# A gated cross-attention and mixture-of-experts layer on one core: the calls of four engines are put in another order

## What is computed

```python
A   = sigmoid(sim) * (sim >= k_th_largest_of_row(sim, 153))      # sim from ctx, Wq, Wk: 512 x 512
adj = (1 - g) * layernorm(x) + g * 0.5 * (A + A.T)
x1  = x + tanh(gx) * adj
xn  = layernorm(x1)
probs = softmax(xn @ gate_w); take the best two of 8 experts per row, weigh them
h   = gelu(xn @ fc1[e] + b1[e]);  y = h @ fc2[e] + b2[e]          # per expert
out = x1 + tanh(gf) * sum over the two experts of weight * alpha[e] * y
```

## Time and profile before

| What | Value |
|---|---|
| Median of 3 runs | 364.33 us (362.4 to 364.58) |
| Profiled execution, its own time | 362.98 us |
| Span of that execution | 361.2 us |
| Mean granted TensorE clock | 0.956 |
| Busy share PE, PEld, DVE, ACT, POOL | 90%, 65%, 55%, 46%, 28% |

### The profile page before, as it was taken

The page is one execution under the profiler, slowest core; times in us unless marked ns, Lnnn a source line. Parts: engine busy times, 40 slices in busy tenths (PEclk is TensorE's granted clock), DMA queues, the critical chain, the costliest instruction groups (busy, mean ns, idle before and its releaser), DMA issues.

```text
span 361.2 us, 6213 instructions
## 1 busy us (share of the span) xinstructions
PE 324.1 (90%) x1969; PEld 234.2 (65%) x1969; DVE 200.2 (55%) x697; ACT 165.2 (46%) x384; POOL 100.0 (28%) x141
## 2 busy tenths in 40 slices
PE   7626998969999998999999989999999999999970
PEld 6303774867765865668868576777785867587720
DVE  0788798887878787698885372636206112311010
ACT  2776336489987656057786222232222212231320
POOL 5001011450111266214307413222733111312131
PEclk9956898989999999999999999999999999999995
DMA  3999999958965686866527766854688955544243
GB/s 91 381 392 362 363 360 382 367 185 189 301 121 154 133 243 210 154 133 197 103 54 188 193 144 139 205 117 91 197 169 153 172 125 105 107 69 86 31 69 54
DMA packets 53637, 65.81 MB, mean 182 GB/s; under 512 B 9792, under 2 KB 28512, under 8 KB 53600
## 3 DMA queue, kind: packets, MB, share of 16 engines
q1 hardware_dynamic: 46144, 47.99, 43.8%
q0 software_dynamic: 7456, 17.37, 24.9%
HBM read 39.56 MB, written 25.78 MB: 181 GB/s over the span
## 4 chain that ended last, share of the span: by engine, by line
PE 44%; issue 19%; DMA 10%; DVE 9%; POOL 5%; ACT 4%; DVEq 3%; POOLq 2%; SPq 1%; ACTq 0%
PE ps L1711 18%; PE ps L1684 14%; PE ps L1694 10%; POOL xs_rows L566 4%; DMA out_rows<-ab,dst 3%; DMA xs_rows<-ab,pos 2%; DMA xg_r<-xs_rows 2%; DMA meta<-xs_rows 2%; ACT ab L692 2%; DMA out_rows<-ys,dst 1%; ACT xb L722 1%; SPq L397 1%; PE ps L1721 1%; PE ps L1647 1%; POOLq L530 1%
## 5 line engine op out<-in xcount | busy, mean ns | idle before, releaser
L1684 PE MATMUL ps<-xgT_r,weights 128*128 128x128 f32 x768 | 91.6, 279 | 6.0 <-ACT xgT_r L743 3.5
L1684 PEld LDWEIGHTS ps<-xgT_r,weights 128*128 128x128 f32 x768 | 89.6, 195 | 11.0 <-issue 8.3
L1711 PE MATMUL ps<-weights,act_r 128*128 128x512 f32 x192 | 86.1, 595 | 1.2 <-ACT act_r L766 1.2
L580 POOL DMA_INDIRECT out_rows<-ys,dst x24 | 37.6, 1568 | 119.1 <-ACT ys L773 64.9
L1711 PEld LDWEIGHTS ps<-weights,act_r 128*128 128x128 f32 x192 | 34.9, 190 | 38.0 <-issue 36.5
L766 ACT ACTIVATE act_r<-ps,b1T 128x128 f32<-128x128 f32 x96 | 27.3, 366 | 37.8 <-PE ps L1684 37.7
L1694 PEld LDWEIGHTS ps<-sim,weights 128*128 128x128 f32 x256 | 35.2, 190 | 1.9 <-issue 1.9
L566 POOL DMA_INDIRECT xs_rows<-ab,pos x32 | 32.0, 1001 | 14.5 <-issue 9.1
L1694 PE MATMUL ps<-sim,weights 128*128 128x160 f32 x256 | 35.6, 299 | 0.0
L773 ACT ACTIVATE ys<-ys,meta 128x512 f32<-128x512 f32 x24 | 17.3, 719 | 34.7 <-DVE ys L1322 34.7
L1711 PE MATMUL ps<-weights,xb 128*128 128x512 f32 x64 | 28.1, 592 | 0.0
(11 more groups left out here) (206 smaller groups left out, 417.8 us busy)
## 6 DMA issues: line engine op xcount, KB each, us to landing
weights<-in_L_ffn_fc_w SPq DMA_DIRECT2D x16, 1024.0 KB, 8.7
b_r<-in_L_ffn_fc_b SPq DMA_DIRECT2D x32, 256.0 KB, 4.0
xg_r<-xs_rows SPq DMA_DIRECT2D x88, 64.0 KB
xb<-in_x SPq DMA_DIRECT2D x4, 1024.0 KB, 7.2
out_rows<-xb SPq DMA_DIRECT2D x4, 1024.0 KB, 5.9
sim<-xs_rows SPq DMA_DIRECT2D x32, 80.0 KB
xs_rows<-weights SPq DMA_DIRECT2D x1, 2064.0 KB, 13.1
xs_rows<-weights SPq DMA_DIRECT2D x2, 516.0 KB, 5.8
```

The lines of the kernel that those rows point to most:

```text
L580: pool.indirect_dma_start(out=out_rows, out_offset=bass.IndirectOffsetOnAxis(ap=dst[:, k % 2, e:e + 1], axis=0), in_=result_rows(m), in_of ...
L1684: mm = pe.matmul(ps[:, n % 2, i * P:(i + 1) * P], weights[:, e, 0, h, i * P:(i + 1) * P], rows[:, h * P:(h + 1) * P], start=(h == 0), stop ...
L1711: mm = pe.matmul(ps[:, 2 + m % 2, :], rows, weights[:, e, 1, i, :], start=(i == 0), stop=(i == IB - 1))
```

## The change

The lists of DVE, ACT, POOL and SP are replaced by others with the same calls; on PE nothing moves. Loops over the four tiles are written out so that calls can stand between them. Parts of the heads of the four lists (SP, POOL, ACT, DVE):

```diff
             load_b2(0, 0)
+            store_x1(0)
+            load_weights(6)
+            load_weights(7)
+            load_x(2)
+            load_meta(0)
             load_b2(0, 1)
-            store_x1(0)
-            fill_pads()
-            load_weights(6)
-            load_x(2)
-            load_weights(7)
-            load_meta(0)
             load_rows(0, 2)
             load_rows(0, 3)
+            fill_pads()
             fill_ends()
             load_rows(0, 4)
+            load_rows(0, 5)
+            load_rows(0, 6)
             load_b2(0, 2)
-            load_rows(0, 5)
             load_b2(0, 3)
-            load_rows(0, 6)
+            load_rows(0, 7)
             load_b2(0, 4)
             store_x1(1)
+            load_x(3)
             load_b2(0, 5)
-            load_rows(0, 7)
-            load_x(3)
             load_b2(0, 6)
+            load_rows(1, 0)
+            load_rows(1, 1)
+            load_rows(1, 2)
+            load_meta(1)
             load_b2(0, 7)
             load_b2(1, 0)
-            load_meta(1)
-            for t in range(3):
-                load_rows(1, t)
...
             rstd_of_x(0)
             rstd_of_x1(0)
+            scatter_rows(0, 0)
+            scatter_rows(0, 1)
+            scatter_rows(0, 2)
+            scatter_rows(0, 3)
             rstd_of_x(1)
-            for t in range(BT):
-                scatter_rows(0, t)
-            rstd_of_x(2)
-            for t in range(3):
-                add_result(0, t)
+            add_result(0, 0)
+            add_result(0, 1)
+            add_result(0, 2)
             rstd_of_x1(1)
             add_result(0, 3)
+            rstd_of_x(2)
+            scatter_rows(1, 0)
+            scatter_rows(1, 1)
+            scatter_rows(1, 2)
+            scatter_rows(1, 3)
             add_result(0, 4)
-            for t in range(BT):
-                scatter_rows(1, t)
             add_result(0, 5)
             add_result(0, 6)
             add_result(0, 7)
+            rstd_of_x1(2)
             add_result(1, 0)
+            add_result(1, 1)
             rstd_of_x(3)
-            rstd_of_x1(2)
...
             act.wait_ge(m_ps, 1)
             act.copy(m_qk[:], ps[:, 0, 0:C]).then_inc(m_sb, 1)
             context(0)
+            query(0)
+            scores(0, 0)
+            scores(0, 1)
+            scores(0, 2)
+            scores(0, 3)
+            squash(0, 0)
+            context(1)
             tanh_coefs()
-            query(0)
-            for t in range(BT):
-                scores(0, t)
-            for t in range(BT):
-                squash(0, t)
-            keep_b1()
             signs(0, 0)
+            signs(0, 1)
+            signs(0, 2)
+            squash(0, 1)
+            squash(0, 2)
+            query(1)
+            squash(0, 3)
             halve(0, 0)
...
-                turned(0, t)
+            turned(0, 0)
+            turned(0, 1)
+            turned(0, 2)
+            turned(0, 3)
             norm_plain(0)
+            signs(1, 0)
             norm_plain(1)
+            scores(2, 0)
+            keep_b1()
+            leaning(0)
+            scores(2, 1)
+            scores(2, 2)
             norm_plain(2)
             norm_plain(3)
-            scores(2, 0)
-            scores(2, 1)
-            leaning(0)
-            scores(2, 2)
             scores(2, 3)
             context(3)
-            for t in range(BT):
-                affine_x(1, t)
-            query(3)
-            signs(1, 0)
+            signs(1, 1)
             picked(0)
             picked(1)
-            signs(1, 1)
+            signs(1, 2)
             gelu(0, 0)
-            signs(1, 2)
+            candidates(1, 0)
+            candidates(1, 1)
+            query(3)
             gelu(0, 1)
+            candidates(1, 2)
+            candidates(1, 3)
+            squash(1, 0)
             signs(2, 0)
...
+            sim_stats(0, 0)
+            sim_stats(0, 1)
+            x_stats(0, 0)
+            sim_stats(0, 2)
+            sim_stats(0, 3)
+            first_guess(0)
+            count(0, 0)
+            narrow(0, 0)
             coefficients()
-            x_stats(0, 0)
-            for t in range(BT):
-                sim_stats(0, t)
-            first_guess(0)
-            keep_gate_sum()
-            count(0, 0)
-            x_stats(0, 1)
-            narrow(0, 0)
             count(0, 1)
-            x_stats(0, 2)
             narrow(0, 1)
             count(0, 2)
+            x_stats(0, 1)
+            x_stats(0, 2)
             x_stats(0, 3)
+            narrow(0, 2)
             x_var(0)
-            narrow(0, 2)
+            keep_gate_sum()
+            largest(0, 0)
+            largest(0, 1)
+            largest(0, 2)
+            largest(0, 3)
...
+            add(0, 2)
+            add(0, 3)
+            x1_stats(0, 0)
+            x1_stats(0, 1)
+            sim_stats(1, 2)
+            x1_stats(0, 2)
+            x1_stats(0, 3)
+            sim_stats(1, 3)
             x1_var_of(0)
-            x_stats(1, 2)
-            x_stats(1, 3)
+            first_guess(1)
             norm_bias(0)
+            best_two(0)
             norm(0, 0)
             norm(0, 1)
-            best_two(0)
             norm(0, 2)
             norm(0, 3)
-            x_var(1)
-            sim_stats(1, 0)
+            one_hot(0)
             gaps(0)
-            sim_stats(1, 1)
-            one_hot(0)
+            sim_stats(2, 0)
+            one_hot(1)
             shares(0)
-            one_hot(1)
             places(0)
-            next_places(0)
-            x_scales(1)
-            sim_stats(1, 2)
-            sim_stats(1, 3)
-            first_guess(1)
-            for t in range(BT):
-                sim_stats(2, t)
+            sim_stats(2, 1)
+            sim_stats(2, 2)
+            sim_stats(2, 3)
             first_guess(2)
             narrow(1, 0)
-            for t in range(BT):
-                x_stats(2, t)
-            x_var(2)
+            x_stats(1, 0)
...
```

462 lines of the change are left out of this document (257 added, 205 removed).

## The result

The changed kernel takes 374.45 us (median of 4 runs, 373.6 to 376.31), the kernel before 363.67 (362.4 to 364.58). The ratio is 1.0299 with an interval of 1.0257 to 1.0340: 3% slower, where 365 was forecast and 369.5 was the end of the range. The profiled execution took 373.6; its span is 371.8, 10.6 longer than before. In the experiments, times are medians of all runs, while ratios leave out the profiled execution and runs more than 1.5% above the fastest of the rest.

What follows compares the result with a forecast made beforehand. PE, busy for 90% of the span, was taken as the bound. Terms -2.3 - 1.6 + 6.1 - 1.6 + 0.9 = +1.5 gave 364.5 from the profiled 362.98, 365.8 from the median; predicted 365 us, range 360 to 369.5.

Steps and rivals of the forecast that it cites:

- part 2: From the first expert product to batch 1's first product: late POOL adds and scatter turn PE's -3.9 us into +2.2.
- part 1: Up to the first expert product at 75.21: start 2.3 us earlier, full clock saves 1.6, PE 3.9 ahead.
- part 3: From 149.57 to 212.12: windows turned before PE asks, so the 1.64 us gap goes, leaving PE at +0.6.
- part 4: From 212.12 to the end: layer2(2, 7) waits 0.9 us because add_bias(21) stands behind turn_rows(3, 0); +0.9.
- the sign: At batch 1's first product: PE 5 us or more behind would show that the landings failed.
- The price of the drain: On POOL ahead of batch 1's scatter: rstd_of_x(2)'s drain waits 5.9 us for the add's landing; bounds 0 and 7.87.
- The start of the adds: On POOL before batch 1's scatter: third add at 114.4 instead of 113.72, fourth at about 126.8.
- lead of 2.7 us: PE's 3.9 us lead from the head, about 1.2 of it lost by the transposed tile after layer2(0, 4).
- B: Adds between 113 and 150 land in 7.87 us, batch 1's product 4 to 6 later: 369 to 371; chance 0.17.
- C: Clock falls again behind the new 3.3 us gap at batch 1's products: 1.6 us, giving 366.6; chance 0.15.
- D: Lists don't do what the title says: copies precede affine passes but stay behind two counts; no separate chance.
- Catch up by the sixth add: Near the end: POOL's adds are one later and catch up by the sixth add of batch 3.

Runs made afterwards that it cites:

- e1: Changed kernel with rstd_of_x(2) moved back behind rstd_of_x(1) on POOL, ahead of the fourth add; 373.49 us, ratio 1.0236.
- e8: e1 with load_meta(3) ahead of store_x1(3) on SP and targets(3) ahead of add_bias(24) on DVE; 369.1 us, ratio 1.0155.
- e11: Changed kernel with only load_meta(3) ahead of store_x1(3) on SP and targets(3) ahead of add_bias(24) on DVE; 374.24 us, ratio 1.0297.
- e14: Changed kernel with narrow(2, 1) ahead of turn_rows(0, 4) on DVE; 376.3 us, ratio 1.0330.
- e3: Changed kernel with 20 matmuls on constants between the second and third transposed tile of adjacency(1, t) on PE; 377.04 us, ratio 1.0343.
- e4: Changed kernel with add_bias(21) moved back ahead of turn_rows(3, 0) on DVE; 377.37 us, ratio 1.0372.
- e10: Changed kernel with ACT's head reordered: norm_plain and two scores calls ahead of signs(1, 0), two picked calls ahead of signs(1, 1); 374.34 us, one run.
- e7: Kernel before with a bare POOL drain added between add_result(0, 4) and the scatter of batch 1; 368.56 us, ratio 1.0164.
- e13: Changed kernel with the first four weigh calls, weigh(0, 0) to weigh(0, 3), moved earlier on ACT; 371.24 us, ratio 1.0146.
- e15: Changed kernel with the moves of both e13 and e14; 368.84 us, ratio 1.0111.

## Why the prediction was wrong

The step that failed is the walk of POOL's adds in part 2 ("I walk to 114.4", "`add_result(0, 3)` starts at about 126.8", "the scatter starts at **132.7**"). Its mechanism was right and shown: the drain of `rstd_of_x(2)` waits for the fourth add, the scatter is late, PE idles. Its sizes were not. The scatter started at 138.01, 5.3 us later than forecast; from there to the product it took the 19.06 us of the forecast. So part 2's term, +6.1 in the sum, came out at +9.4 (from -1.95 at `layer2(0, 0)` to +7.5 at `layer1(1, 0)`). The sum also lacked a lower clock behind that (+1.7), and the other parts missed by less: part 1 gave -1.95 instead of -3.9, part 3 -0.6 instead of -1.6, part 4 +1.9 instead of +0.9. The prediction had named the sign: PE 5 us or more behind at that point means that the landings failed.

- **The price of the drain, 3.7 of the 5.3 us.** I took 5.9 after an add's start. The bare drain took 5.98, but in the changed kernel it was 9.59, since the add landed in 8.6 us; the slowest of the 34 adds before the change took 7.1 (the one at 202.44). Why this one took 8.6 stays open. The load of x beside it isn't enough: in the kernel before, the same load went out 1.48 us behind the same add (121.54), and that add landed in 4.9. The transfers there from 121 to 126:

```profile
xb<-in_x SPq DMA_DIRECT2D x1, 1024.0 KB, 6.8
out_rows<-ys,dst POOLq DMA_INDIRECT x1, 4.9
```

  In the new order the load goes out 1.09 us behind the add, with two bias loads behind it, and in e1, e8, e11 and e14, where that is the same, the add took 7.2 to 7.5. What of this makes it slow was not tried apart.
- **The start of the adds, 1.6 of the 5.3 us.** The third came at 117.06 instead of 114.4, the fourth at 128.42 instead of 126.8. Both rows name ACT, and no landing, as what ended POOL's wait, so that the first add came 8.7 us later than before held up neither. `weigh(0, 2)` waited behind the copy (L743) of a transposed tile, and that for PE, on whose lead of 2.7 us (3.9 less 1.2) the walk counted there. PE came to the tile at 114.94 and before the change at 115.01: 2.0 us of the lead had not been won in part 1, and the way to the tile had cost 1.9 instead of 1.2, the gap above all. From the third add the delay passed on to `leaning(1)`, which ran at 127.32 instead of 125.6, and with it to the fourth. PE before and after, and ACT after:

```profile
115.01 1.04 PE L1639 MATMUL ps<-ident,xb 128*128 128x128 f32 x8
```

```profile
114.94 1.06 PE L1717 MATMUL ps<-ident,xb 128*128 128x128 f32 x8
```

```profile
115.57 0.58 ACT L743 COPY x1T<-ps 128x512 f32<-128x512 f32 x1 [5.30 <-PE ps L1717]
116.06 0.72 ACT L786 ACTIVATE ys<-ys,meta 128x512 f32<-128x512 f32 x1
...
127.32 0.21 ACT L760 ACTIVATE lean<-gap 128x4 f32<-128x4 f32 x1 [5.13 <-DVEq L1238]
```

- **Rivals B and C came together with the forecast's mechanism.** I gave each a chance as if only one could come. B (a landing over 6.8 us) took place at the one landing that mattered; three adds of the kernel before had already been over that or at it (7.1, 6.9 and 6.8). C's clock fell behind the gap ahead of `layer1(1, 0)` (9.15 us for 64 matmuls, 1.66 more than before, as priced) and once more from 119.6, where I had none, for 3.2. The latter is no pure loss: without it (e14) PE only waits longer for the scatter. The Trainium skill, "TensorE: Matmul & The Clock Gate", section "The HAM clock gate", lets an idle engine fall back. The profiles agree for gaps of 4.43 to 4.76 us at this place (8.65 to 9.38 us for the 64 matmuls in the changed kernel, e3, e4, e10 and e11), and for the 3.54 of the earlier trace rows; behind 3.10 and 3.27 (e14, e7) the clock stayed up (7.31, 7.41). Behind the shorter gap ahead of 110 it fell in six of nine profiles, so the length of a gap alone doesn't tell.
- **Part 1** gave 1.95 of 3.9. The clock's 1.6 came (64 matmuls in 7.38 us); the earlier start didn't. The proof was read at 38.46, 1.4 earlier than before instead of 2.6, and the reciprocal root was asked for 1.0 later (54.04 against 53.06) instead of 0.2 to 0.4 earlier. Picking ran from 64.67 at a clock of 0.80, and `narrow(1, 0)` ended at 71.0 instead of 69.2, so the copies ended late and the product started at 74.89. The first copies were behind two counts, as D said. And e10 shows that an earlier start would have been worth nothing, since the GELU stands behind the next count.
- **Part 3.** The gap of 1.64 us became 0.44 (-1.2 of the 1.6 forecast), and new gaps, 0.65 at most, took half of it.
- **Part 4.** The wait of `layer2(2, 7)` was 1.36 instead of 0.9, right in kind (e4). "Catch up by the sixth add" held in the profiled execution, but it used up all slack of the adds, and I had named no row for that slack: gains on PE were lost at the end in e1, e13 and e15.

The Trainium skill, "DMA: Bandwidth & Descriptors", section "Anatomy of one DMA — SWDGE (gpsimd) path", would have put the landing at an estimate of 2.6 us. The 34 adds of the changed kernel took 4.7 to 8.6; the trace differs and decides.

## What to carry to other kernels

Before an operation with a drain is put behind a transfer on the same engine, ask who waits behind the drain, and price it by the slowest landing in the stretch where it will stand, not by a row from another stretch alone. Carry a lead forward in the sum only to calls where something shows that it is still there; here 2.7 us of it had gone before the first wait that counted on it. Where adds each wait for the last landing, the place of the first and the slack at the end are terms of the sum, with rows of their own. And rivals that share a cause (a late transfer, a gap, a lower clock) add up.

## What was not expected of the hardware

- A drain on POOL with no computation ahead of it waits for an indirect transfer in flight: 5.98 us from the add's start to the next instruction (e7), where it was 1.90 without the drain.
- One form of transfer, a 256 KB indirect add, took 4.6 to 7.1 us to land before the change and 4.7 to 8.6 after it. The same 1 MB load went out 1.48 us behind one that landed in 4.9, and 1.09 us behind the one that took 8.6.
- The granted clock from 111 to 127 us fell to 0.5 to 0.6 in seven of 17 profiled executions of kernels with one and the same list on PE (e3's 20 matmuls apart), in one of them behind a gap of only 0.44 us.
